# A new order for batch 0's projections and for the output products of the merged stages, in a kernel of four chained cross-attention blocks

## The reference

```python
# L0: projections of z and ctx, 16 heads of 64, then Wo, residual, norm over channels
h = W_i @ z[:, :, s:e] + Winj_i @ ctx[:, :, s:e]          # two halves of 128 positions
q, k, v = split(h);  rq = q + r_w_bias
x = Wo @ (softmax(rq^T k / 8) v) + bo + z;  x = (x - mean) * rsqrt(var + 1e-5)
# L1: attention of x (latents) over [ctx, x] with a mask, 16 heads of 16; rmsnorm; gelu MLP
# L2: layer norm, attention of x over ctx with a mask, 16 heads of 16; layer norm; gelu MLP
# L3: attention over ctx, 16 heads of 8: mean and standard deviation of v under the weights,
#     then instance norm of x, times the deviation, plus the mean
```

## Time and profile before

| | |
|---|---|
| time, three runs | 1088.85 us median (1088.43 to 1091.02) |
| profiled execution | 1090.98 us, span 1089.2 us |
| TensorE busy | 969.2 us (89% of the span) |
| VectorE busy | 541.8 us (50%) |
| ScalarE busy | 485.7 us (45%) |
| GpSimd busy | 270.3 us (25%) |

### The profile page before, as it was taken

The page is one execution under the profiler, slowest core; times in us unless marked ns, Lnnn a source line. Parts: engine busy times, 40 slices in busy tenths (PEclk is TensorE's granted clock), DMA queues, the critical chain, the costliest instruction groups (busy, mean ns, idle before and its releaser), DMA issues.

```text
span 1089.2 us, 21560 instructions
## 1 busy us (share of the span) xinstructions
PE 969.2 (89%) x8592; PEld 604.7 (56%) x8592; DVE 541.8 (50%) x1028; ACT 485.7 (45%) x937; POOL 270.3 (25%) x389
## 2 busy tenths in 40 slices
PE   7789999999999989999999999999999999975771
PEld 6456664666546664566636664556646665344520
DVE  2443565445645465445644556455654556453340
ACT  1424444454544545445544535345454455333233
POOL 0230220243202521223302422116202332024103
PEclk9899999999999999999999999999999999988876
DMA  9300221002300203102300013002110022002001
GB/s 370 137 2 1 78 89 30 24 2 84 106 28 8 79 7 105 35 2 83 105 17 20 30 54 107 30 6 83 45 67 32 2 83 97 18 18 77 5 5 35
DMA packets 29059, 60.15 MB, mean 55 GB/s; under 512 B 9377, under 2 KB 21025, under 8 KB 24097
## 3 DMA queue, kind: packets, MB, share of 16 engines
q1 hardware_dynamic: 28960, 58.77, 14.9%
HBM read 53.52 MB, written 5.24 MB: 54 GB/s over the span
## 4 chain that ended last, share of the span: by engine, by line
PE 74%; issue 10%; DVE 10%; ACT 4%; POOL 2%; DMA 1%; POOLq 0%; SPq 0%; DVEq 0%; ACTq 0%
PE GP L583 6%; PE GP L988 6%; PE PV L722 6%; PE GP L999 6%; PE GP L585 5%; PE SC L705 4%; DVE nm L1426 4%; PE SC L797 4%; PE GP L972 3%; PE PV L768 3%; PE GP L814 3%; PE SC L906 3%; PE GP L590 2%; PE PV L919 2%; PE GP L591 2%
## 5 line engine op out<-in xcount | busy, mean ns | idle before, releaser
L1426 DVE TENSOR_REDUCE nm<-MX 128x2 bf16<-128x512 f32 (+1 forms) x352 | 227.1, 689 | 162.6 <-PE MX L644 65.6
L1216 ACT ACTIVATE Pr<-SC,bcol 128x512 f32<-128x512 f32 x128 | 80.9, 683 | 134.2 <-PE SC L797 134.2
L1755 POOL TENSOR_TENSOR Psum<-Pr 128x512 f32<-128x512 f32 x56 | 71.3, 1274 | 169.4 <-ACT Pr L1214 169.4
L583 PE MATMUL GP<-zP,W 128*128 128x128 f32 x512 | 106.1, 289 | 7.6 <-DMA W<-w 7.6
L1214 ACT ACTIVATE Pr<-SC 128x512 f32<-128x512 f32 x128 | 69.3, 593 | 82.1 <-PE SC L705 82.1
L585 PE MATMUL GP<-uP,W 128*128 128x128 f32 x512 | 99.8, 277 | 0.0
L583 PEld LDWEIGHTS GP<-zP,W 128*128 128x128 f32 x512 | 78.4, 193 | 27.8 <-issue 26.1
L1244 ACT ACTIVATE Pr<-SC,bcol 128x512 f32<-128x512 f32 x96 | 60.7, 684 | 58.2 <-PE SC L906 58.2
L1723 POOL TENSOR_TENSOR stat<-stat,half 128x1 f32<-128x1 f32 x24 | 13.7, 569 | 269.0 <-DVE stat L1602 172.7
L585 PEld LDWEIGHTS GP<-uP,W 128*128 128x128 f32 x512 | 78.6, 194 | 0.0
L999 PE MATMUL GP<-WB,work 128*128 128x256 f32 x256 | 62.5, 394 | 10.5 <-DVE work L1550 10.5
(11 more groups left out here) (194 smaller groups left out, 1730.9 us busy)
## 6 DMA issues: line engine op xcount, KB each, us to landing
WA<-w1a SPq DMA_DIRECT2D x8, 1024.0 KB, 4.8
WB<-w1b SPq DMA_DIRECT2D x8, 1024.0 KB, 7.0
WA<-w2a SPq DMA_DIRECT2D x8, 1024.0 KB, 4.9
WB<-w2b SPq DMA_DIRECT2D x8, 1024.0 KB, 7.1
W<-w SPq DMA_DIRECT2D x6, 1024.0 KB, 10.4
scratch<-U SPq DMA_DIRECT2D x16, 256.0 KB, 2.0
C<-scratch SPq DMA_DIRECT2D x96, 32.0 KB
zP<-z_in SPq DMA_DIRECT2D x8, 128.0 KB, 4.4
```

Of the source, the lines that this page charges most:

```text
L583: pe.matmul(dst, W0[:, piece, 2 * s, at:at + P], zP[:, s * P:s * P + P], start=True, stop=False)
L1216: act.activation(Pr[:, (n + j) % 4, :], SC[j], ACT.Exp, bias=bcol[:, 3 + k % 2:4 + k % 2], scale=8.0 ** -0.5).then_inc(p_ready, 1)
L1426: dve.tensor_reduce(dst, MX[(n + i) % 2][:].rearrange("p (a k) -> p a k", a=a), AX_X, ALU.max, negate=True).then_inc(mx_done, 1)
L1755: pool.tensor_tensor(Psum[:, c % 4, :].rearrange("p (a l) -> p a l", l=D), two[:, :, 0:D], two[:, :, D:2 * D], ALU.add)\
```

## The change

Batch 0: `PROJ` becomes q, k, q, k, v, v and so on; only four projections stand ahead of the first maxima product, two lie inside `EARLY`, and the rest are dealt out over steps 0 to 4 by `START`, on all three engines. The weight pieces are loaded in the order 0, 2, 4, 1, 3, 5, with identity, masks and selectors behind piece 2 still. The wait for constants moves to the first transpose. ScalarE's casts follow the projections they need.

Merged stage: out0 to out3 go together behind `pv3(b, 2)`, out4 and out5 behind `pv3(b, 4)`, out6 and out7 behind `pv3(b, 6)`. In `mix_end` the second half of kp0 comes before `pv3(b, 7)`.

```diff
-        (3, 2, [(0, 1, "B"), ("recip", 1, 1)], [("out", 0), (3, 2, 0)]),
-        (3, 3, [("out", 1), (3, 2, 2)], [("out", 2), ("out", 3), (3, 2, "T")]),
+        (3, 2, [(0, 1, "B"), ("recip", 1, 1)], [(3, 2, 0)]),
+        (3, 3, [(3, 2, 2)], [*(("out", c) for c in range(4)), (3, 2, "T")]),
         (3, 4, [(0, 2, "B")], [(3, 3, 0)]),
-        (3, 5, [(3, 3, 2), ("out", 4)], [("out", 5), (3, 3, "T")]),
-        (3, 6, [(0, 3, "B")], []), (3, 7, [("out", 6), ("out", 7)], [])]
+        (3, 5, [(3, 3, 2)], [("out", 4), ("out", 5), (3, 3, "T")]),
+        (3, 6, [(0, 3, "B")], []), (3, 7, [], [("out", 6), ("out", 7)])]
...
+PROJ = ["qp0", "kp0", "qp1", "kp1", "vp0", "vp1", "qp2", "kp2", "qp3", "kp3", "vp2", "vp3"]
+START = {0: ("qp2", "kp2"), 1: ("qp3",), 2: ("kp3",), 3: ("vp2",), 4: ("vp3",)}
...
-            for i in range(6):
+            for i in (0, 2, 4, 1, 3, 5):
...
+                    if b < 0:
+                        for name in START.get(k, ()):
+                            project(name, prologue, 0)
...
                     transpose_x0(b + 1)
-                    pv3(b, 7)
                     if more:
                         project("kp0", order_of(b + 1), b + 2, (2, 3))
+                    pv3(b, 7)
...
-            for name in PROJ:
+            for name in PROJ[:4]:
                 project(name, prologue, 0)
-            pe.wait_ge(const_v, 2)
-            pe.wait_ge(const_p, 3)
-            pe.wait_ge(ld_par, 48)
             make = {0: maxima0(0)}
-            for _, g, u in EARLY:
+            for (_, g, u), name in zip(EARLY, ("vp0", "vp1", None, None)):
+                if u == "T" and g == 0:
+                    pe.wait_ge(const_v, 2)
+                    pe.wait_ge(const_p, 3)
+                    pe.wait_ge(ld_par, 48)
                 make[0](g, u)
+                if name:
+                    project(name, prologue, 0)
...
-                    if b < 0 and k == 0:
-                        cast(0, 2)
...
+                    if b < 0:
+                        for name in START.get(k, ()):
+                            if name[0] != "q":
+                                project(name, prologue)
+                        if k in (0, 2):
+                            cast(0, 2 + k // 2)
...
-            for name in PROJ[4:]:
-                project(name, prologue)
+            for g in range(2):
+                project(f"kp{g}", prologue)
+                cast(0, g)
...
+            for v in ("vp0", "vp1"):
+                project(v, prologue)
```

More of the change, by code:

```diff
@@ L156 @@
 F_STEPS = 6
-PROJ = [f"qp{i}" for i in range(4)] + [f"kp{i}" for i in range(4)] + [f"vp{i}" for i in range(4)]
+PROJ = ["qp0", "kp0", "qp1", "kp1", "vp0", "vp1", "qp2", "kp2", "qp3", "kp3", "vp2", "vp3"]
+START = {0: ("qp2", "kp2"), 1: ("qp3",), 2: ("kp3",), 3: ("vp2",), 4: ("vp3",)}
 BODY = ["kp0", "kp1", "q1", "k1", "v1", "qp0", "kp2", "qp1", "vp0", "o1", "vp1", "oT", "m0", "m1", "k2",
@@ L1222, in mixed @@
                         queries3(b, [(Q3b, 2), (Q3b, 3), (Q3, 2), (Q3, 3)])
-                    if b < 0 and k == 1:
-                        cast(0, 3)
                     if L == 0 and (k in (4, 6) or k == 2 and b < 0):
                         evacuate(b + 1, k // 2 - 1)
+                    if b < 0:
[4 more added lines that the diff above has]
+                            cast(0, 2 + k // 2)
                     if L == 3 and k == 4:
@@ L1374, in _ @@
             act.wait_ge(ld_cols, 16)
-            cast(0, 0)
-            cast(0, 1)
+            for v in ("vp0", "vp1"):
+                project(v, prologue)
             mixed(-1, range(8))
@@ L1446, in mixed @@
                         unit(*name)
+                    if b < 0:
+                        for name in START.get(k, ()):
+                            if name[0] == "q":
+                                project(name, prologue)
                     if b < 0 and k == 5:
@@ L1669, in _ @@
             dve.wait_ge(ld_cols, 16)
-            for name in PROJ[:4]:
+            for name in ("qp0", "qp1"):
                 project(name, prologue)
```

## The result

| | before | changed |
|---|---|---|
| median | 1089.37 us (1087.70 to 1091.71, 20 runs) | 1091.94 us (1090.34 to 1097.84, 20 runs) |
| ratio | | 1.0032, interval 1.0022 to 1.0041 |
| profiled execution's span | 1089.2 us | 1092.3 us |
| TensorE busy in it | 969.2 us | 965.7 us |

The change costs 0.32%, 3.5 us by the ratio. The mean times differ by 3.4, the medians by 2.6: three of the 20 executions of the changed kernel took 1097.7 to 1097.8 us. By the stages of the two profiles, the kernel has won some 6 us in the head and lost some 8 in the seven merged stages. The first view of the changed kernel is the busy time by stretch (columns as in rows 1).

What follows compares the result with a forecast made beforehand. TensorE was taken as nearly full, with VectorE's and ScalarE's chains binding where products moved. Head -6.2, stages +3.5, kp0 +4.2, seventh +0.5 gave +2.0 on 1088.85: 1090.8 us, range 1084.5 to 1095.5.

Steps and rivals of the forecast that it cites:

- Head, -6.2: Batch 0's first attention: projections dealt between the pieces fill most of an 8.7 us hole, -6.2 us.
- a head that gives little: Rival, batch 0: ScalarE's casts and exponentials pace each step, 3 us of the hole stay; 1093.9 us, chance 0.13.
- Group of four, +0.6 per stage: Merged stages, group 2: VectorE's chain makes moving out0 and out1 behind pv3(2) delay the transpose, +0.6 us each.
- 0.4 and 0.6: Merged stages: expected waits in us before the first and second maxima product of group 2, where none was.
- TensorE is the bound everywhere: Rival: VectorE's chain gives way, groups bring 0.6 us per stage; about 1077 us, chance 0.18 with a half-way case.
- the pair of out4 and out5: Merged stages, behind pv3(4): joining these two output products brings -0.1 us per stage.
- Split kp0, +0.7 in six stages: End of six merged stages: kp0's second half ahead of pv3(7) delays pv3(7) and so q1, +0.7 us each.
- ScalarE alone binds q1: End of the merged stages with kp0: q1 follows pv3(7)'s start by 3.48 us through ScalarE's copies and moment sums.
- Seventh stage: Last merged stage, without kp0: out6 and out7 behind pv3(6) come later, +0.5 us, beside +0.6 and -0.1.
- Low clock in the stages: Rival: new waits in merged stages make TensorE's clock fall; 1102.7 us with one fall per stage, chance 0.07.
- the price of 1.7 us: Merged stages: cost of each fall of TensorE's clock, read from a q1 taking 4.54 us instead of 2.89.

Runs made afterwards that it cites:

- e1: Only batch 0's new order and load order, merged stages as before, against the kernel before: 1083.46 us, ratio 0.9945.
- e11: Changed kernel with the weight pieces loaded in their old order 0 to 5: 1094.46 us, ratio 1.0046 to the kernel before.
- e3: Kernel before with only the second half of kp0 moved ahead of pv3(7): 1096.00 us, ratio 1.0055.
- e2: Kernel before with only the output products regrouped in four, two and two: 1092.98 us, ratio 1.0028.
- e10: Changed kernel with ScalarE's three moment sums between its copies of kp0 and kp1: 1091.19 us, ratio 1.0019 to the kernel before.
- e5: Changed kernel with out0 and out1 put back ahead of group 2's maxima products: 1089.16 us, ratio 0.9999 to the kernel before.
- e7: Kernel before with batch 0's new order and, in six stages, pv3(7) right behind pv3(6), then x0 transposes and whole kp0: 1080.27 us, ratio 0.9915.
- e8: e7 with out4 and out5 together behind pv3(4): 1080.05 us, ratio 0.9914 to the kernel before.
- e6: Changed kernel with L3's group 2 row maxima taken over half of the keys: 1088.99 us, ratio 0.9991 to the kernel before.

## Why the prediction was right, and where it was short

The forecast was 1090.8, +2.0; measured +3.5 by the ratio (2.4 to 4.5), at the edge of the 0.3% I called no change. The time itself, 1091.94, is 1.1 above the forecast; half of that is the base, 1088.85 from three runs where twenty give 1089.37. By its steps:

- **Head, -6.2.** Right: -6.0 by e1. Piece 2 was the load that mattered: with the old order it costs a wait of 1.43 (e11), where I had 1.7; for piece 4 e11 shows no wait at all, where I had 1. No wait for ScalarE stands between the first maxima product and step 5, so it did not pace the steps, and the rival of a head that gives little fell.
- **Group of four, +0.6 per stage.** Right in kind and nearly in size: +0.53. Waits of 0.42 and 0.48 came where 0.4 and 0.6 were named. The rival in which TensorE is the bound everywhere asked for a gain of 0.6. Its premise holds (each change of kind costs TensorE some 0.1: in the changed kernel four output products and one entry are 1.83, in the earlier trace rows one with two sides 0.64), and TensorE's work did shrink: from the stage's start to q1 it is busy 25.18 us in place of 25.70, with 224 matmul records in both. What it saved turned into waits, but for the pair of out4 and out5, where no wait lay: -0.10, as forecast. (The whole profile's fall from 969.2 to 965.7 us is no proof of this: e1, with the old order of output products, has 965.3, as the head's low clock is gone there too.)
- **Split kp0, +0.7 in six stages.** Right: pv3(7) at 319.55, stage + 25.01, where the old order with the same delay ahead of it would be at 24.27 (23.84 + 0.43); 3.49 to q1, kp1's wait 0.74. Taken alone the split costs 0.90 (e3), and the output products 0.28 in place of 0.5 (e2): the 0.2 that out6 and out7 save beside kp0 stands in the forecast's 0.7 and, by the experiments, with the output products. The sum of both in a stage is +1.18; forecast 1.2. That ScalarE alone binds q1 held only just: by e10 the chain through kp1 is just 0.2 shorter.
- **Seventh stage.** +1.01 in all; forecast 0.5 + 0.5. The transposes waited 0.75 in place of 0.18, q1 2.17 in both.
- **Low clock in the stages.** Did not come: 1.00 from 60 to 900 us. The prediction reads the 4.54 of q1 in the earlier trace rows as a q1 at 1.2 GHz. The granted clock fell at 956.4 us, a microsecond into it, so only the rest was at the lower level; the price of 1.7 us stays as it was.

So the stages sum to 7.2 for the six and 1.0 for the seventh, +8.2 as forecast, and with -6.0 the kernel should stand at +2.2. The three comparisons of the changed kernel say 3.5, 3.8 and 3.9. **What stays open** is this 1.3 to 1.7 us, about as large as one interval but of the same sign three times. By the medians the three say 2.57, 3.55 and 3.75. A part lies in a few long executions: four of the 32 of the changed kernel took 1097.7 to 1098.1 us at a mean clock of 0.970, while none of the kernel before took more than 1092.4, even at 0.968. No profile shows such an execution, and where its time goes stays open. e5, whose stages and head sum to 6 x 0.65 + 0.47 - 6.0 = -1.6, came out at -0.1, while e7 (-6.0 - 6 x 0.5 = -9.0; measured -9.3) has no excess. It is not in the stages, which agree within 0.05 us in each profile of a kernel. Between the last q1 and the end of the span the profiles differ by more than that, with the clock. These are the stretches of e1 and of the changed kernel's first profile:

```profile
950.54:1081.20 130.66, 78.18 (x660) 47.21 (x660) 48.34 (x92) 41.49 (x78) 33.06 (x56) 0.82 0.08 28
957.05:1092.30 135.25, 82.82 (x660) 49.33 (x660) 48.35 (x92) 41.52 (x78) 32.60 (x56) 0.77 0.08 27
```

Both hold the same 660 matmul records. In all fourteen profiles the length of this stretch follows its mean clock: 130.7 to 130.9 us at 0.81 or 0.82 (e1, e7, e11), 133.0 to 133.8 at 0.78 (eight profiles, among them before with 133.8 and the changed kernel with 133.0 and 133.4), 134.2 to 135.3 at 0.77 (e8, e2 and the changed kernel's first). Where the gaps of the last batch meet low clock, the time moves by as much as what is missing.

Whether the changed kernel meets more of it on the average, the mean clock of every execution can tell in part. It is 0.9728 over the 56 executions of the kernel before that were timed beside the experiments, and 0.9760 over the six of e1, whose head no longer has the low stretch of the earlier trace rows. The changed kernel has that head too, and yet its 32 executions stand at 0.9735. The missing 0.0025 of 1090 us, at half speed, is an estimated 5 us more at the lower level, and as no profile with the new head shows a fall before the last batch, that is where it is likely to lie. In the two stretches above, the changed kernel has an estimated 15 us more of the lower level than e1 (62 against 47, from their clocks) and is 4.6 us longer; at that rate 5 us are worth about 1.6, the size of what is open. This is an estimate and no proof: e8 stands at 0.973 too and came out only 0.4 above its sum, and why the changed kernel meets more low clock was not shown. The sum on the record had no term for the last batch.

## What to carry to other kernels

A short product that stands between two steps of another engine's chain is a cover: before moving it, write down when the product behind it could start without it. If the answer is "at the same time", moving it saves only its change of kind and costs its whole length where it goes. The same holds at a hand-over: an instruction that frees a buffer for the other engine's queue (here pv3(7)) is worth pulling forward ahead of filler work, above all where it then stands beside a product of its own kind, as in e7, where the joining saved the half microsecond. And a change in several parts is to be timed in its parts: here a part worth -6 us was shipped with two worth +9.

## What the runs showed of the hardware

The last batch, without fillers, took between 130.7 and 135.3 us from its q1 to the end in fourteen profiles, all but one (e6, whose reductions are shorter) with the same instructions in it; in the packed stages the three profiles of the changed kernel differ by 0.05 us. One execution's span is therefore no measure of a change of 0.3% here; the length of a stage at clock 1.00 is.
The Trainium skill, page "TensorE: Matmul & The Clock Gate", section "What's actually happening", says that by default the clock is throttled and activity releases it. The trace agrees: the granted clock rose only after TensorE had begun to work, at 10.2 to 13.6 us in thirteen profiles, and at 16.1 in e11, where a wait of 1.43 us came first.
